# Two attention layers over eight images: layer 0 computed in the transposed layout, values fed tile by tile

## The reference, cut to what matters

```python
# layer 0
q = einsum('oc,bcn->bno', Wq, xf) + bq          # 32 channels
k = einsum('oc,bcn->bon', Wk, xf) + bk          # 32 channels
v = einsum('oc,bcn->bon', Wv, xf) + bv          # 256 channels
attn = softmax(einsum('bnc,bcm->bnm', q, k), axis=-1)
x = gamma[0] * einsum('bcj,bij->bci', v, attn) + x
# layer 1
h = group_norm(x, 32 groups)
q, k, v = 1x1 convolutions of h, 256 channels each
attn = softmax(einsum('bct,bcs->bts', q, k) / 16, axis=-1)
x = x + proj(einsum('bcs,bst->bct', v, attn))
```

## Time and profile before

| | before |
|---|---|
| runs, us | 850.29, 851.35, 851.42; median 851.35 |
| span of the profiled execution, us | 852.3 |
| PE busy | 805.0 us (94%), 4076 matmuls |
| DVE busy | 536.9 us (63%) |
| ACT busy | 476.2 us (56%) |
| GpSimd busy | 194.3 us (23%) |
| DMA | 18.6 MB, 22 GB/s over the span |

### The profile page before, as it was taken

One profiled execution on the slowest core, in us unless ns is written; L12 is line 12 of the kernel. 1 busy time (PEld: TensorE's weight loads), 2 busy tenths in 40 slices (PEclk: granted clock), 3 DMA queues, 4 the chain that ended last, 5 costly groups with the idle time before them and its releaser, 6 DMA issues.

```text
span 852.3 us, 11428 instructions
## 1 busy us (share of the span) xinstructions
PE 805.0 (94%) x4076; PEld 674.3 (79%) x4076; DVE 536.9 (63%) x814; ACT 476.2 (56%) x609; POOL 194.3 (23%) x181
## 2 busy tenths in 40 slices
PE   4589889999999999999999999999999999999898
PEld 3477777888877888788878888778887888887776
DVE  5645566765677665775667656776657756563482
ACT  3662865566644765557555676447655575542261
POOL 1001613040420414113330404204141133104300
PEclk9979799999999999999999999999999999999999
DMA  5000000000200001000200002000010000000001
GB/s 173 1 1 1 11 40 1 0 25 1 74 0 0 25 25 49 0 0 25 74 0 0 25 0 74 0 0 25 25 49 0 0 25 26 1 1 25 25 1 50
DMA packets 10339, 18.62 MB, mean 22 GB/s; under 512 B 2128, under 2 KB 3920, under 8 KB 10320
## 3 DMA queue, kind: packets, MB, share of 16 engines
q1 hardware_dynamic: 10320, 18.36, 6.2%
HBM read 9.97 MB, written 8.39 MB: 22 GB/s over the span
## 4 chain that ended last, share of the span: by engine, by line
PE 67%; DVE 18%; ACT 8%; issue 6%; DMA 1%; DVEq 0%; SPq 0%; ACTq 0%
PE pv_ps L477 10%; PE pv_ps L478 10%; PE pv_ps L479 10%; PE ring L477 9%; PE ring L479 9%; PE ring L478 9%; PE pt_ps L511 6%; DVE neg_raw L891 5%; ACT prob L686 3%; PE ring L496 3%; DVE x L836 2%; DVE bn L839 1%; DVE k L814 1%; DVE k L812 1%; DVE pt_lo L872 1%
## 5 line engine op out<-in xcount | busy, mean ns | idle before, releaser
L686 ACT ACTIVATE prob<-ring,neg_max 128x1024 f32<-128x1024 f32 x128 | 143.0, 1117 | 131.1 <-DVE neg_max L892 94.3
L477 PE MATMUL pv_ps<-pt_hi,v_hi 128*128 128x512 f32 x512 | 202.0, 394 | 0.5 <-DVE pt_lo L872 0.3
L478 PE MATMUL pv_ps<-pt_lo,v_hi 128*128 128x512 f32 x512 | 200.5, 392 | 0.0
L479 PE MATMUL pv_ps<-pt_hi,v_lo 128*128 128x512 f32 x512 | 200.3, 391 | 0.0
L891 DVE TENSOR_REDUCE neg_raw<-ring 128x1 f32<-128x1024 f32 x64 | 78.1, 1220 | 76.3 <-PE ring L479 72.0
L662 ACT ACTIVATE pt_hi<-prob,row_inv 128x1024 fp32r<-128x1024 f32 x64 | 73.8, 1153 | 80.6 <-DVE row_inv L879 77.3
L477 PE MATMUL ring<-h_hi,query_hi 128*128 128x512 f32 x256 | 103.1, 403 | 13.5 <-ACT prob L686 13.5
L889 DVE TENSOR_REDUCE neg_max<-ring 128x1 f32<-128x1024 f32 x64 | 78.4, 1225 | 59.2 <-PE ring L496 58.3
L477 PEld LDWEIGHTS pv_ps<-pt_hi,v_hi 128*128 128x128 f32 x512 | 96.7, 189 | 20.9 <-DVE pt_lo L872 1.1
L479 PEld LDWEIGHTS pv_ps<-pt_hi,v_lo 128*128 128x128 f32 x512 | 96.5, 188 | 21.0
L478 PEld LDWEIGHTS pv_ps<-pt_lo,v_hi 128*128 128x128 f32 x512 | 96.7, 189 | 18.5
(11 more groups left out here) (103 smaller groups left out, 1267.0 us busy)
## 6 DMA issues: line engine op xcount, KB each, us to landing
out_y<-res SPq DMA_DIRECT2D x32, 256.0 KB, 2.1
x_in<-in_x SPq DMA_DIRECT2D x7, 1024.0 KB, 4.9
x_in<-in_x SPq DMA_DIRECT2D x2, 512.0 KB, 4.9
h_f<-in_wv_t SPq DMA_DIRECT2D x1, 256.0 KB, 5.0
res<-in_wq SPq DMA_DIRECT2D x1, 256.0 KB, 5.0
res<-in_wk SPq DMA_DIRECT2D x1, 256.0 KB, 5.3
res<-in_wv SPq DMA_DIRECT2D x1, 256.0 KB, 5.5
res<-in_wp_t SPq DMA_DIRECT2D x1, 256.0 KB, 5.5
```

What stands on the lines that cost most here:

```text
L477: mm(out, w_hi, m_hi, start=first, stop=False)
L478: mm(out, w_hi, m_lo, start=False, stop=False)
L479: return mm(out, w_lo, m_hi, start=False, stop=last)
L686: activation(prob[:, k % 2], ring[:, slot], ACT.Exp, bias=neg_max[:, k % 2:k % 2 + 1], accum_out=row_sum[:, k % 2:k % 2 + 1]).then_inc(S[" ...
```

## The change

What it does:

- Layer 0 gets its probabilities directly in the transposed layout. First, one image ahead, each of the eight tiles is computed in rows ("scores"): DVE takes the maximum, ACT the exponential, in place in the ring, only for its row sum. From maximum and sum comes one number a row, shift = -max - ln(sum) (ACT takes the logarithm of all eight columns at once, DVE makes a hi and lo pair). Eight small matmuls against a float32r identity move the shifts to a row ("shift"), and ACT copies them to partitions 96 and 97 of `q4`, beside ones in `k4`. Then each tile is computed again with the roles of q and k exchanged ("keys"): the matmul adds the shift, and the exponential is the finished, transposed probability. ACT copies it to `pt_hi`, DVE makes `pt_lo` from two tiles in SBUF. Transposes, `pt_ps`, the identity's use and the scaling of layer 0 are gone.
- The two banks of `pt_ps` go to `pv_ps`: four accumulators. The values take each tile once, two steps after it is made, 12 matmuls over the four banks.
- `q4` and `k4` have 96 (98) rows in place of 128, and are there twice; so is `x_in`; `prob` has three buffers, `pt_hi` and `pt_lo` four of one tile each, `v1_f` its own memory.
- Image 0 goes through scores and keys first; while its values run, image 1 gets its scores, and after them its first keys. The second half of this turn has no layer-1 tiles.
- GpSimd splits x of image i + 2 ahead of h of image i. The DMA of x for image 1 is issued ahead of the layer-1 weights.
- All turns are written out; there is no loop on any engine.

The core of the diff:

```diff
-PV_LAG = 6
+PROBS = 3
+PT = 4
+BANKS = CT * HALVES
...
+def head():
+    steps = [Step() for _ in range(10)]
+    steps[0].sides = [("qk", 0, 0), ("qk", 0, 1), ("value0", 0, 0), ("value0", 0, 1)]
+    for k in range(TILES):
+        steps[1 + k].late = [("scores", 0, k)]
+    steps[9].log = 0
+    steps[9].sides = [("value0", 0, 2), ("value0", 0, 3)]
+    steps[9].late = [("shift", 0, 0)]
     return steps
...
+def turn(i):
+
+    steps = [Step() for _ in range(2 * TILES)]
+    has = lambda image: 0 <= image < IMAGES
+    for s, step in enumerate(steps):
+        if s < TILES and has(i) and not (i == 1 and s < 2):
+            step.tile = ("keys", i, s)
+        if s >= TILES and has(i - 1):
+            step.tile = ("logits", i - 1, s - TILES)
+        back = (s - 2) % (2 * TILES)
+        layer, image = back // TILES, i - back // TILES - (s < 2)
+        if has(image):
+            step.values = [(layer, image, back % TILES)]
+    if i == 0:
+        steps[0].split_x = 1
+        steps[1].sides = [("weights", 0, 0)]
+        steps[3].sides = [("qk", 1, 0), ("qk", 1, 1)]
+        steps[5].sides = [("bias", 0, 0)]
+        for k, s in enumerate((4, 5, 6, 7, 8, 8, 9, 9)):
+            steps[s].late.append(("scores", 1, k))
+        steps[10].log = 1
+        steps[11].late.append(("shift", 1, 0))
+        steps[13].tile, steps[14].tile = ("keys", 1, 0), ("keys", 1, 1)
+    elif has(i + 1):
+        steps[2].sides += [("qk", i + 1, 0), ("qk", i + 1, 1)]
+        for k in range(TILES):
+            steps[6 + k].late.append(("scores", i + 1, k))
+        steps[14].log = i + 1
+        steps[15].late.append(("shift", i + 1, 0))
+    if has(i - 1):
+        steps[0].hidden = i - 1
+        for m in range(2):
+            steps[3 + m].sides.append(("query", i - 1, m))
+        for m in range(4):
+            steps[5 + m // 2].sides.append(("value1", i - 1, m))
+    if has(i + 1):
+        for m in range(4):
+            steps[10 + m].sides.append(("value0", i + 1, m))
+    if has(i):
+        for m in range(2):
+            steps[11 + m].late.append(("norm", i, m))
+    if has(i + 2):
+        steps[14].split_x = i + 2
+    return steps
...
+        pv_ps = ctx.enter_context(nc.psum_tensor("pv_ps", [P, BANKS, HALF], F32))
...
+            for i in range(IMAGES):
+                coefficients(i)
+                if i + 2 < IMAGES:
+                    split_x(i + 2)
+                split_hidden(i)
+                residual1(i)
+                if i + 1 < IMAGES:
+                    residual0(i + 1)
+                for m in range(4):
+                    split_value1(i, m)
...
+            def scores(i, k, out):
+                if k == 0:
+                    wait("qk_split", 2 * i + 2)
+                rows = slice(k * P, (k + 1) * P)
+                for cols in half_cols:
+                    last = mm(out[:, cols], q4[i % 2][0:96, rows], k4[i % 2][0:96, cols], start=True, stop=True)
+                return last
+
+            def keys(i, k, out):
+                if k == 0:
+                    wait("shift_read", i + 1)
+                rows = slice(k * P, (k + 1) * P)
+                for cols in half_cols:
+                    last = mm(out[:, cols], k4[i % 2][0:98, rows], q4[i % 2][0:98, cols], start=True, stop=True)
+                return last
...
+            def move_shift(i, out):
+                wait("shift_ready", i + 1)
+                for k in range(TILES):
+                    last = mm(out[0:2, k * P:(k + 1) * P], shift_pair[:, k], ident_r[:], start=True, stop=True)
+                return last
...
+            def fill(now, entry):
+                kind, i, m = entry
+                n, slot = now.ring[entry], now.slot[entry]
+                out = ring[:, slot]
+                if n >= 2:
+                    wait(*reader(SLOT_OF[n - 2]))
...
+            def values(layer, i, k):
+                p, phase = TILE_NO[bool(layer), i, k], PHASE_NO[layer, i]
+                v_hi, v_lo = ((v0_hi, v0_lo), (v1_hi, v1_lo))[layer]
+                if k == 0:
+                    wait(("value0_split", "value1_split")[layer], 4 * i + 4)
+                wait("p_split", p + 1)
+                for b, (half, ct) in enumerate(bank_of):
+                    if k == 0 and phase > 0:
+                        wait("pv_read", (phase - 1) * BANKS + b + 1)
+                    w, cols = slice(ct * P, (ct + 1) * P), half_cols[half]
+                    last = three(pv_ps[:, b], v_hi[:, k, w], v_lo[:, k, w], pt_hi[p % PT][:, cols],
+                                 pt_lo[p % PT][:, cols], k == 0, k == TILES - 1)
...
+            for now in STEPS:
+                if now.tile:
+                    fill(now, now.tile)
+                for entry in now.sides:
+                    fill(now, entry)
+                for tile in now.values:
+                    values(*tile)
+                for entry in now.late:
+                    fill(now, entry)
...
+            def row_sums(now, entry):
+                _, i, k = entry
+                slot = now.slot[entry]
+                act.wait_ge(S["scores_max"], i * TILES + k + 1)
+                activation(ring[:, slot], ring[:, slot], ACT.Exp, bias=neg_max0[:, k:k + 1],
+                           accum_out=row_sum0[:, k:k + 1]).then_inc(S["scores_exp"], 1)
...
+            def log_sums(i):
+                act.wait_ge(S["scores_exp"], (i + 1) * TILES)
+                activation(log_sum0[:], row_sum0[:], ACT.Ln).then_inc(S["log_ready"], 1)
+
+            def shift_rows(now, entry):
+                _, i, _ = entry
+                act.wait_ge(S["ring_ready"], now.ring[entry] + 1)
+                copy(q4[i % 2][96:98], ring[0:2, now.slot[entry]]).then_inc(S["shift_read"], 1)
...
+            for now in STEPS:
+                if now.log is not None:
+                    log_sums(now.log)
+                if now.hidden is not None:
+                    hidden(now.hidden)
+                if now.tile:
+                    exponent(now)
+                    if now.tile[0] == "keys":
+                        prob_hi(now.tile)
+                for entry in now.sides:
+                    project_hi(now, entry)
+                if now.tile and now.tile[0] == "logits":
+                    prob_hi(now.tile)
+                for entry in now.late:
+                    if entry[0] == "scores":
+                        row_sums(now, entry)
+                    if entry[0] == "shift":
+                        shift_rows(now, entry)
+                if now.split_x is not None:
+                    split_x(now.split_x)
...
+            for now in STEPS:
+                if now.log is not None:
+                    shifts(now.log)
+                if now.evacuate:
+                    evacuate(*now.evacuate)
+                if now.tile and now.tile[0] == "logits":
+                    row_max(now, now.tile)
+                if pending:
+                    prob_lo(pending)
+                    pending = None
+                for entry in now.sides:
+                    project_lo(now, entry)
+                if now.tile and now.tile[0] == "keys":
+                    prob_lo(now.tile)
+                if now.tile and now.tile[0] == "logits":
+                    row_inverse(now.tile)
+                    pending = now.tile
+                for entry in now.late:
+                    if entry[0] == "scores":
+                        row_max(now, entry)
+                    if entry[0] == "norm":
+                        norm(now, entry)
+                if now.evacuate and now.evacuate[0] == 0:
+                    statistics(now.evacuate[1])
```

More of the change, by code:

```diff
@@ L53 @@
 VW = C + 2
[L57 to L69, removed]
@@ L134, in __init__ @@
         self.slot = {}
+        self.ring = {}
     def entries(self):
[L137 to L146, removed]
-    t = (s - PV_LAG) % STEPS
-    part = there((t // TILES, t % TILES // 4, t % 4), 0 if s >= PV_LAG else -1)
-    step = Step(tile(0), [(kind, m) for kind, m in ITEMS.get(s, []) if has(IMAGE_OF[kind])],
-                [part] if part else [], values_first=s == VALUES_FIRST,
-                h=(s,) if s < CT and has(-1) else (), load_x=s == TILES and has(1),
-                block0=s == 2 and has(-2))
-    step.previous, step.old = tile(1), tile(2)
-    step.late = [item for item in step.items if s == 2 or item == ("norm", 0)]
-    return step
@@ L161, in take_slots @@
-def take_slots(steps, first):
-    n = first
-    for step in steps:
-        for entry in step.entries():
-            step.slot[entry] = n % 2
-            n += 1
-    return steps
-def span(*turns):
-    return [regular(lambda d: 0 <= i + d < IMAGES, s) for i, steps in turns for s in steps]
-FIRST = 3
-HEAD = span((-1, (10, 11, 12)), (0, range(STEPS)), (1, range(PV_LAG)))
-HEAD[FIRST + 14].items.insert(0, ("bias", 0))
-for _step in HEAD:
-    _step.hi_first = True
-take_slots(HEAD, 0)
-TURNS = IMAGES - 2
@@ new lines @@
+STEPS = head() + [step for i in range(IMAGES + 2) for step in turn(i)]
```

(40 more changed lines are left out.)

893 lines of the change are left out of this document (357 added, 536 removed).

## The result

The changed kernel takes 934.35 us (median of four runs, 933.47 to 935.56), the kernel before 850.82 us beside it (849.30 to 851.42): a ratio of 1.098, interval 1.095 to 1.101. It is slower by 83 us. The profiled execution spans 932.4 us, where the one before spans 852.3.

The account below looks back on a forecast made before the run. PE's matmul queue, without slack, bounds the kernel: 95.7 us of work plus waits 4.9, 2.7, 2.0, 2.0 and 0.4 of handovers make 107.7 a turn against 99.41; with head and end 912.8, so 912 us, range 878 to 942.

Parts of the forecast that it names:

- (a): Steps 11 and 12: after norm, the next logits wait for the slot of the scores just issued; 2.45 us twice, 4.9.
- (b): End of step 15: keys 0 of the next turn waits for ACT's copy of the shift; 2.7 us, bounds 1.3 to 4.
- the walk: Step-by-step reckoning of the steady turn, 107.7 us; as a case 890 to 935 us in all, chance 0.68.
- the rival of a falling clock: One ten-us stretch at 1.2 GHz in each of six turns: +5 us a turn, 943 us; chance 0.12.
- the four signs of being wrong: Steps 12, 13 logits unwaited; keys 0 within 1 us of shift; clock under 1.00 after 120 us; turn under 102.
- PE work: Steady turn's matmuls: transposes -6.3, second layer-0 pass +4.4, shift +0.8; from 96.8 to 95.7 us, a gain of 1.1.
- (c): Step 2, two qk projections: keys 3 waits 0.5 us and the first query matmul 1.5; 2.0 us a turn.
- (d): Steps 9 to 11: layer-0 work queues in DVE ahead of the logits' maximum; four small waits, 2.0 us a turn.
- Head: Before image 0's first query: bare row pass and later waits put it at 128.5 us, 25 later; bounds 117 to 137.
- The end: Image 6's to image 7's query 82.5 us against 84.4; from there to the end 60.4 against 69.4.
- Shared port: DVE's lo colliding with GpSimd: nothing outside the shift wait; without cover up to 1 us for each of some three tiles.
- Covers: Evacuation of layer 1 hidden by keys and qk, that of layer 0 by logits and value0; no wait counted.

## Why the prediction was right, and where its sizes were off

Direction and range held: 934 lies in 878 to 942. The forecast of 912 was 22 us low, 60 us more than before in place of 80 by the profiled executions. Of the 19.6 us between the forecast's 912.8 and the profiled 932.4, 6.5 are the head, 10.4 the six turns and 2.6 the end. The three large waits were where they were forecast, at about their sizes, and taking (a) and (b) away gave back 49 us, so the mechanism held. The number is less good than it looks: 934 is at the upper edge of the walk's own 890 to 935 and nearer to the rival of a falling clock (943) than to 912. And of the four signs of being wrong, one came: the clock is 0.97 in steady turns, after 120 us.

- **PE work.** Taken as -6.3 + 4.4 + 0.8. Eight shift matmuls take 0.48 us (bounds 0 to 0.8), two score or keys matmuls 0.47 in place of 0.54, sixteen times a turn. The sign was right, the gain some 1.4 us a turn larger, about 2.5.
- **(a) Norm.** 2.45 us twice forecast. The second stop is the 2.44 us of the row above, the first 2.05. Confirmed by moving norm: 29 us in all.
- **(b) Shift.** 2.7 forecast. From the shift to keys are 3.83 us, less its own 0.48 = 3.35; the chain is the forecast one with the collision in it. Of the 0.65 more, 0.3 are the shorter shift, the rest small handovers. Within its bounds. Confirmed by moving the shift.
- **(c) qk.** 2.0 forecast, 0.4 + 1.6 measured from start to start. Two tries to take it away made others.
- **(d) Steps 9 to 11.** 2.0 forecast, 1.1 measured (0.24, 0.58 and 0.29).
- **Clock.** This is the step that the sum had wrong. I gave it as a rival of its own with one long stretch a turn, +5 us and 0.12, and counted nothing in the sum. It came in every turn, smaller: the values behind the shift's stop take 4.11 in place of 2.74 us, the query behind the stop for qk 4.44 in place of 2.90 at full clock, 2.9 us a turn, 17 in all. That is more than the 10.4 by which the six turns were under-reckoned: a turn at full clock would be 106.3, so the waits and the work alone were 1.4 us over-reckoned (more gain in PE work and shorter waits in (d), partly offset by (b)). That the turn came out within 1.5 us of the forecast is in this part luck. The clock fell behind stops of 3.2 and 1.4 us and not behind those of 2.0 and 2.4 in the same turn; in the turn looked at with the shift moved it was the norm stops that it fell behind. The Trainium skill ("TensorE: Matmul & The Clock Gate", A second HAM failure mode) has short idle gaps between bursts bring the half rate back; the trace agrees behind two of the four stops. The effect deserved to be a term of the sum rather than one chance in eight.
- **Head.** +25 forecast, +31 measured. The row pass ended at 36.0, as forecast. Behind it the bias matmuls took 6.9 us at half clock where I had 3.5, and PE stood 4.0 us for h. That the row pass is its largest piece is shown by leaving it out (17 us). The rest was not taken apart: PE stands 4.2 us for x of image 2 ahead of its qk and 4.0 for h of image 0, and putting h first gained 4 us that the displaced qk took back.
- **The end.** From image 6's to image 7's query 82.6, forecast 82.5. After it 63.0 in place of 60.4: the query there ran at half clock.
- **Shared port.** Counted at nothing outside (b). Shown to be so for residuals and value1; for the split of x it is a part of (b) and was not separated.
- **Covers.** "The evacuation of layer 1 is covered by keys and qk" was shown by taking qk away: a stop of 2.9 us a turn.

What stays open: why the clock falls behind some of these stops and not behind others, and how much of the head's remaining 14 us belongs to which handover.

## What to carry to other kernels

With a ring of two slots, write down for every fill what PE does between the last fill of that slot and this one; if it is less than the trip through the readers (3.2 us here), PE stands still by the difference, and swapping two entries can be worth more than the whole idea of the change: here 29 us against some 2.5 us a turn of matmul work that the two layouts saved. Count a short stop in a busy queue at more than its length, since the matmuls behind it may run at half clock. And before moving work out of a place, ask what it covers: both tries to cure the wait for qk uncovered or made another. The one edit here that beats the kernel before is none of this change's: smaller pieces on GpSimd, 7 us.

## What the runs showed of the hardware

- TensorE's clock fell from 2.4 to 1.2 GHz behind stops of 1.4 and 3.2 us in each steady turn of the changed kernel, and not behind stops of 2.0 and 2.4 us in the same turns; in a turn of the kernel with the shift moved it fell behind stops of 2.1 and 2.4 us and not behind one of 1.3. Twelve matmuls of 512 columns took 2.7 to 2.9 us at full clock and 4.1 to 5.3 with a drop.
- DVE's lo with two SBUF operands waited for the GpSimd operation under way and then ran before GpSimd's next one: 3.27 us where GpSimd's pieces were of 2.4 us, 2.15 where they were of 1.2, 1.27 with none.
- ACT's copy of 2 partitions x 1024 takes 1.00 us, as long as one of 128 partitions (1.05).
- The exponential written in place into PSUM takes 1.09 us, 1.12 into SBUF, each with 0.19 more to read out the row sum; the logarithm between the exponentials takes 0.21 us.
- Hardware loops on the engines cost 0.3 us a turn here; a program written out in full costs nothing that shows (849.42 against 851.39 us).
